# A new opening for a fused attention and expert kernel: other load order, weights cast in two parts, one modulation product moved into block 0

## The chip, the cores and the metric

The kernel runs on one core of one Trainium2 chip. The metric is the time of one execution on the device in microseconds (us), the median of several runs. TensorE is called PE here, VectorE DVE, ScalarE ACT, GpSimd POOL, and SyncE SP. SP only issues DMAs.

## What is computed

```python
mod = (silu(c) @ wmod).reshape(4, 6, 1, -1)          # six modules of 512 columns for each of 4 batches
sa, ca, ga, sb, cb, gb = (mod[:, k] for k in range(6))
h = layernorm(x) * (1 + ca) + sa                     # x: 4 x 2048 x 512
xn = rmsnorm(h) * gamma
q, kv, a = split(xn @ w_qkva.T, 3)                   # 512 columns of each kind
s = scan(sigmoid(a), kv)                             # s[t] = a[t] * s[t-1] + kv[t]
x = x + clip(ga) * (q * s)
h = layernorm(x) * (1 + cb) + sb
x = x + clip(gb) * experts(h)                        # 8 experts, top 2, capacity 320 for each batch
```

## The kernel before

The 8192 tokens are cut into 16 **blocks** of 512 tokens, each of 4 tiles of 128 (TB = 4). The first part of the kernel walks over these blocks. The second part runs the experts, and it isn't touched. Each engine has its own instruction list, written out by hand in `build_program`. Engines wait for one another by counting semaphores, so an instruction that waits holds back all that stands behind it on its engine.

**The opening** comes before block 0. SP loads `wmod` in six modules of 1 MB, the first block of x (1 MB) and the four quarters of the projection weights `wq` (768 KB each). For each module m, `mod_mm(m)` on PE multiplies silu(c) with it (four products, which the profile shows as eight matmuls, since they are fp32), and `mod_copy(m)` on ACT (or one DVE instruction for module 1) takes the row out of PSUM. Modules 1 and 0 are then spread over all partitions by `mod_spread`, and copied from PSUM to `mods`. Module 2 is the gate `ga`, modules 3 and 4 serve the second norm, and module 5 is the gate `gb`, needed by the experts.

ACT's `stats1` computes a block's means (`nm1`) and variances, POOL's `rstd1` takes the inverse root (`rs1`), and DVE's `apply1` makes the normed rows `h1` in two parts: part 0 needs `nm1` and module 1, part 1 needs `rs1` and module 0. ACT's `square` sums the squares of `h1`, POOL's `rnorm1` takes the inverse root, ACT's `hi1` and DVE's `lo1` write the rows as a high and a low fp16 half, and SP's `turn_x` transposes them by DMA (one for each tile) into `xns`.

The weights are cast in the same two halves. DVE's `wq_max` finds the maximum of each quarter; a short exchange over PE (two small products into bank 7) and a chain of small DVE instructions make the scale `gsc`; ACT writes the high halves `wqs[:, 0]`, DVE the low ones.

**A block** on PE is twelve calls of `qkv`, numbered k = 0 to 11: for each quarter c = k // 3 of the 512 columns, the kinds a, kv and q, each of 12 fp16 matmuls of 512 columns. Kind a writes the one bank `bank_a`, and so waits until ACT's `sigmoid` of the quarter before has read it: call k = 6 waits for the second sigmoid. DVE's `mix(c)` is the scan over the block and the product with q; `cga`, the gate, is a factor of that product. For the gate, DVE's `gate(2)` clips module 2, PE's `turn_gate` turns it, and DVE's `gates_done` scales it. The function `step` of each engine gives the order inside a block:

```
ACT, block 0: sigmoid(0), square(block 1), sigmoid(1), hi1(block 1), sigmoid(2), sigmoid(3), stats1(block 2)
DVE, block 0: apply1(block 1, part 0), apply1(block 1, part 1), gates_done, mix(0), lo1(block 1), mix(1), mix(2), mix(3), gate(5)
```

Of the kernel before, what the change touches and what calls it, by code (L numbers as in the profile page):

```python
# [20 lines left out]
P = 128  # L21
# [28 lines left out]
MOD_BANK = {0: 6, 1: 5, 2: 2, 3: 3, 4: 4, 5: 1}  # L50
ROW_DONE = {1: 1, 0: 2, 2: 3, 3: 4, 4: 5, 5: 6}
WQ_LINKS = 12
# [28 lines left out]
def build_program(nc, x, gamma, wq, wr, w1, b1, w2, b2, ct, wmod, out):  # L81
# [4 lines left out]
    with ExitStack() as ctx:  # L86
# [23 lines left out]
        wmod_hi = reg_b[:, :].bitcast(F32)[:, 2 * 2048:].rearrange("p (q n) -> p q n", q=2)  # L110
# [24 lines left out]
        wq_raw = reg_e[:, 2 * TB * D:2 * TB * D + KC * 3 * D].rearrange("p (c e) -> p c e", c=KC)  # L135
        modt = reg_e[:, TB * D:TB * D + 2 * D]
# [388 lines left out]
        def _(sp):  # L525
# [57 lines left out]
            def step(q, j, i):  # L583
                n = 4 * q + j
                if i == 0:
                    for e in range(E // 2):
                        fill(e, 0)
                    turn_x(0, 1)
                    for e in range(E // 2, E):
                        fill(e, 0)  # L590
                if i == 1:
                    sp.wait_ge(s_dch, 14)
                    sp.wait_ge(s_mrow1, 1)
                    sp.dma_start(mod_rows[:, 0:2 * D], modr[0:B, 0:2 * D]).then_inc(s_modw, 16)
# [21 lines left out]
                if i == 0:  # L616
                    for c in range(4):
# [102 lines left out]
            sp.wait_ge(s_modmm, ROW_DONE[5])  # L720
# [14 lines left out]
        def _(pool):  # L735
# [25 lines left out]
            def rnorm1(n):  # L761
                wait_alone(pool, s_sq, TB * n + TB)
                wait_alone(pool, s_xlo, TB * n)
                g.tensor_scalar(rn1[:, :], ss1[:, :], 1e-24 / D / XSCALE ** 2, None, ALU.max).then_inc(s_rna, 1)
                wait(pool, s_rna, n + 1)
                g.tensor_tensor(rn1[:, :], rn1[:, :], half[:, :], ALU.pow).then_inc(s_rn, 1)
# [36 lines left out]
            rnorm1(0)  # L803
# [47 lines left out]
        def _(act):  # L851
# [27 lines left out]
            def square(n):  # L879
                wait(act, s_rn, n)  # L880
# [7 lines left out]
            def hi1(n):  # L888
                wait(act, s_xn, 16 * TB * n)
                wait(act, s_rn, n + 1)  # L890
                for t in range(TB):
                    a.activation(xrow[:, t, 0:D], h1[:, t, :], ACT.Copy, scale=rn1[:, t:t + 1]).then_inc(s_xhi, 1)
# [40 lines left out]
            def mod_copy(m):  # L933
                act.wait_ge(s_modmm, ROW_DONE[m])
                if m == 5:
                    act.wait_ge(s_modc, 1)
# [3 lines left out]
            mod_copy(0)  # L940
            act.wait_ge(s_spread, 2)
            a.activation(mods[:, 0, :], bank[0][:, :], ACT.Copy).then_inc(s_mod0, 1)
            square(0)
            hi1(0)
            act.wait_ge(s_wch0, WQ_LINKS - 4)
            for c in range(KC):
                act.wait_ge(s_wqraw[c], 16)
            for c in range(KC):
                a.activation(wqs[:, 0, c, :], wq_raw[:, c, :], ACT.Copy, scale=gsc[:, c:c + 1]).then_inc(s_wqhi, 1)
            for m in range(2, 6):  # L950
                mod_copy(m)
            stats1(0, 1)
            act.wait_ge(s_wch0, WQ_LINKS)

# [7 lines left out]

            def step(q, j, i):
                n = 4 * q + j
                if has(i, 0):
                    sigmoid(n, 0)
# [15 lines left out]
                if has(i, 0):  # L982
                    sigmoid(n, 2)
                    sigmoid(n, 3)
# [194 lines left out]
        def _(dve):  # L1179
# [27 lines left out]
            def apply1(q, j, part):  # L1207

                n = 4 * q + j
                if part == 0:  # L1210
                    wait(dve, s_nm1, 2 * n + 1)
                    wait(dve, s_xlo, TB * n)
                    if j == 0:
                        wait(dve, s_ma, 16 * q)
                    for t in range(TB):
                        v_.scalar_tensor_tensor(h1[:, t, :], xbuf[:, j, t, :], nm1[:, 0, t:t + 1], mods[:, 1, :],
                                                ALU.add, ALU.mult).then_inc(s_a1, 1)
                else:
                    wait(dve, s_r1, n + 1)
                    if n == 0:  # L1220
                        dve.wait_ge(s_mod0, 1)
                    for t in range(TB):
                        wait(dve, s_a1, TB * n + t + 1)
                        v_.scalar_tensor_tensor(h1[:, t, :], h1[:, t, :], rs1[:, t:t + 1], mods[:, 0, :],
# [64 lines left out]
            dve.wait_ge(s_modmm, ROW_DONE[1])  # L1289
            v_.tensor_scalar(modr[0:B, D:2 * D], bank[MOD_BANK[1]][0:B, :], 1.0, None, ALU.add).then_inc(s_mrow1, 1)  # L1290
            dve.wait_ge(s_spread, 1)
            v_.tensor_copy(mods[:, 1, :], bank[1][:, :]).then_inc(s_modc, 1)
            dve.wait_ge(s_modc, 1)
            apply1(0, 0, 0)

# [5 lines left out]

            wq_max(0)
            apply1(0, 0, 1)
            wq_max(1)
            wq_max(2)
            wq_max(3)
# [7 lines left out]
            lo1(0, 1, 2)  # L1314
# [5 lines left out]
            lo1(0, 2, TB)  # L1320
            for c in range(KC):
                dve.wait_ge(s_wqhi, c + 1)
                v_.scalar_tensor_tensor(wqs[:, 1, c, :], wq_raw[:, c, :], gsc[:, c:c + 1], wqs[:, 0, c, :],
                                        ALU.mult, ALU.subtract).then_inc(s_wqlo, 1)
# [6 lines left out]
            dve.wait_ge(s_modc2, 2)  # L1331
            gate(2)
# [108 lines left out]
            def step(q, j, i):  # L1441
# [21 lines left out]
                if i == 0:  # L1463
                    gates_done()
                if has(i, 0) and j == 0:
                    wait(dve, s_y, KC * n)
                    wait(dve, s_cga, 1 if i == 0 else 0)
                    v_.tensor_copy(cga[:, :], gaS[:, :, q]).then_inc(s_cga, 1)
                    wait(dve, s_cga, 2 * q + 2)
                if has(i, 0):  # L1470
# [500 lines left out]
        def _(pe):  # L1971
            mm, tr = nc.tensor.matmul, nc.tensor.transpose
            pe.sem_inc(s_mm2, 1)
            pe.wait_ge(s_cd, 4 * E + 3)
            pe.wait_ge(s_silc, 1)
# [76 lines left out]
            def qkv(q, j, c, kind):  # L2052
# [12 lines left out]
                if n == 0 and c == 0 and kind == 1:  # L2065
                    pe.wait_ge(s_modc2, 5)
# [39 lines left out]
            pe.wait_ge(s_modc, 1)  # L2106
            attn_steps(step)
# [253 lines left out]
```

## Time and profile before

| | |
|---|---|
| median of 3 runs | 2147.0 us (2145.99 to 2148.63) |
| profiled execution, its time | 2147.44 us |
| its span in the trace | 2145.6 us |
| PE busy | 2113.4 us, 98% |
| DVE busy | 1783.2 us, 83% |
| ACT busy | 1061.7 us, 49% |
| POOL busy | 378.9 us, 18% |

Times in the trace count from the span's start. A row of the timeline gives the start, the duration, the engine, the line of the kernel, the operation, what it writes and reads, and the count of instructions merged into the row; behind it, in brackets, stand the idle time before it and what ended that. A matmul's own duration contains its latency; the pace of a row of many is the row's duration by its count.

### The profile page before, as it was taken

The page shows a single profiled execution, that of the slowest core. Times are in us where ns is not written, and L with a number is a line of the kernel's source. Part 1 is how long each engine was busy: PE and PEld are TensorE (multiplying, and loading weights), DVE is VectorE, ACT ScalarE, POOL GpSimd, SP SyncE. Part 2 cuts the span into 40 slices and gives each one's busy share as a digit, 9 for nine tenths or more (in the row PEclk, how much of TensorE's full clock was granted, in tenths as well). Part 3 has the DMA queues.
Part 4 walks back from the last instruction along what each step waited for, and adds up shares of the span by engine and source line. Part 5 has one row for each costly group of instructions (what it writes and reads, how often), then busy time and mean ns, then how long its engine had stood idle before and what let it go on. Part 6 is the DMA issues. An engine that isn't in the chain of part 4 may idle for free.

```text
span 2145.6 us, 35624 instructions
## 1 busy us (share of the span) xinstructions
PE 2113.4 (98%) x13294; PEld 1257.3 (59%) x13294; DVE 1783.2 (83%) x3029; ACT 1061.7 (49%) x2098; POOL 378.9 (18%) x335
## 2 busy tenths in 40 slices
PE   7999999999999999999999999999999999999998
PEld 2454444445474657656764766576466657656676
DVE  7799989999888887887888779778877987887754
ACT  5465666667372645355253625534461644355150
POOL 1034343433423010100001010101101010100101
PEclk9999999999999999999999999999999999999999
DMA  8899996775675742553274345416434551553202
GB/s 292 246 259 249 243 242 158 177 171 126 160 195 142 207 113 60 145 150 100 33 214 117 81 121 150 124 26 192 105 98 100 171 125 49 168 128 99 40 11 26
DMA packets 353213, 301.05 MB, mean 140 GB/s; under 512 B 242476, under 2 KB 242732, under 8 KB 352529
## 3 DMA queue, kind: packets, MB, share of 16 engines
q1 hardware_dynamic: 331136, 256.63, 43.4%
q0 software_dynamic: 21904, 42.14, 10.3%
q8 instruction: 105, 1.72, 0.3%
q14 instruction: 68, 0.55, 0.1%
HBM read 163.84 MB, written 93.01 MB: 120 GB/s over the span
## 4 chain that ended last, share of the span: by engine, by line
PE 93%; DVE 2%; issue 1%; SPq 0%; DMA 0%; ACT 0%; POOLq 0%; DVEq 0%; ACTq 0%
PE bank L2161 32%; PE bank L2077 20%; PE bank L2231 19%; PE bank L2241 9%; PE bank L2268 5%; PE bank L2259 4%; PE bank L2149 2%; PE bank L2026 1%; DMA reg_e<-reg_e 0%; DVE reg_b L1579 0%; PE bank L2037 0%; PE bank L2039 0%; SPq L581 0%; SPq L573 0%; DVE reg_e L1365 0%
## 5 line engine op out<-in xcount | busy, mean ns | idle before, releaser
L2077 PE MATMUL bank<-reg_c 128*128 128x512 f16 x2296 | 505.2, 379 | 1.0 <-ACT reg_e L961 1.0
L2161 PE MATMUL bank<-reg_e,reg_a 128*128 128x320 f16 x2880 | 447.5, 299 | 0.0
L2231 PE MATMUL bank<-reg_b,reg_c 128*128 128x512 f16 x1920 | 417.3, 379 | 0.9 <-DVE reg_b L1579 0.9
L2077 PEld LDWEIGHTS bank<-reg_c 128*128 128x128 f16 x2296 | 222.3, 98 | 258.3 <-ACT reg_e L961 1.5
L2161 PEld LDWEIGHTS bank<-reg_e,reg_a 128*128 128x128 f16 x2880 | 280.9, 98 | 112.7
L2231 PEld LDWEIGHTS bank<-reg_b,reg_c 128*128 128x128 f16 x1920 | 187.3, 98 | 226.1 <-issue 2.3
L845 POOL DMA_INDIRECT out_dram<-reg_e,midx x79 | 138.8, 1757 | 948.1 <-DVE reg_e L1614 875.2
L2161 PE MATMUL bank<-reg_e,reg_d 128*128 128x320 f16 x1440 | 232.5, 299 | 0.0
L1054 ACT ACTIVATE reg_e<-bank,b1s 128x320 f32<-128x320 f32 x120 | 63.3, 528 | 248.8 <-PE bank L2161 247.9
L2161 PEld LDWEIGHTS bank<-reg_e,reg_d 128*128 128x128 f16 x1440 | 139.7, 98 | 57.6 <-ACT reg_e L1054 4.0
L787 POOL DMA_INDIRECT slot_rows<-reg_e,sli x112 | 129.8, 1159 | 101.1 <-DVE reg_e L1439 60.7
L1649 DVE TENSOR_REDUCE wm<-reg_d 128x1 f32<-128x1024 f32 x112 | 135.6, 1210 | 3.1 <-DMA reg_d<-in_w 3.1
L1704 DVE SCALAR_TENSOR_TENSOR reg_e<-bank,reg_e 128x320 f32<-128x320 f32 x120 | 58.9, 491 | 79.3 <-PE bank L2161 78.3
L1611 DVE SCALAR_TENSOR_TENSOR reg_e<-bank,inv,reg_e 128x512 f32<-128x512 f32 (+1 forms) x81 | 59.9, 740 | 73.7 <-PE bank L2268 41.3
L1124 ACT ACTIVATE reg_e<-reg_e 128x2560 f16<-128x2560 f32 x15 | 35.1, 2337 | 169.1 <-DVE reg_e L1773 169.1
L2161 PE MATMUL bank<-reg_e 128*128 128x320 f16 x720 | 117.4, 299 | 0.0
L2268 PE MATMUL bank<-reg_b,reg_c 128*128 128x512 f16 x512 | 114.4, 379 | 0.0
L1082 ACT ACTIVATE reg_c<-reg_e 128x320 f16<-128x320 f32 x120 | 55.9, 466 | 101.1 <-DVE reg_e L1704 101.1
L961 ACT ACTIVATE reg_e<-bank,iq 128x512 f32<-128x512 f32 x60 | 40.9, 681 | 129.8 <-PE bank L2077 91.5
L2259 PE MATMUL bank<-reg_b,reg_c 128*128 128x512 f16 (+1 forms) x432 | 88.2, 355 | 1.4 <-issue 1.4
L2161 PEld LDWEIGHTS bank<-reg_e 128*128 128x128 f16 x720 | 70.4, 98 | 29.5
L1722 DVE SCALAR_TENSOR_TENSOR reg_a<-reg_d,wsc,reg_a 128x1024 f16<-128x1024 f32 x58 | 71.9, 1279 | 16.8 <-ACT reg_a L1096 16.8
(263 smaller groups left out, 3385.9 us busy)
## 6 DMA issues: line engine op xcount, KB each, us to landing
reg_d<-in_w SPq DMA_DIRECT2D x232, 512.0 KB
slot_rows<-zrow SPq DMA_DIRECT2D x32, 516.0 KB, 4.9
reg_b<-in_x SPq DMA_DIRECT2D x16, 1024.0 KB, 7.4
out_dram<-reg_b SPq DMA_DIRECT2D x16, 1024.0 KB, 7.3
reg_d<-in_w SPq DMA_DIRECT2D x8, 1024.0 KB, 9.6
slot_rows<-zrow SPq DMA_DIRECT2D x32, 129.0 KB, 4.8
reg_d<-in_wmod SPq DMA_DIRECT2D x4, 1024.0 KB, 11.8
reg_e<-mod_rows SPq DMA_DIRECT2D x7, 512.0 KB, 9.5
```

What stands on the lines that cost most here:

```text
L787: g.indirect_dma_start(out=rows, out_offset=bass.IndirectOffsetOnAxis(ap=sli[:, pj % 2, k, t:t + 1], axis=0), in_=rowi[:, pj % 2, t, :], i ...
L845: g.indirect_dma_start(out=out, out_offset=bass.IndirectOffsetOnAxis(ap=midx[:, u, t:t + 1], axis=0), in_=yo[:, n % 4, :], in_offset=None, ...
L1054: a.activation(part_of[:, n % 2, :], u_bank, ACT.Identity, bias=ba[:, p:p + 1], scale=HID_SHIFT).then_inc(s_r0, 1)
L1611: v_.scalar_tensor_tensor(yo[:, n % 4, cols], src, inv2[:, u, kind:kind + 1], b2t[:, cols], ALU.mult, ALU.add).then_inc(s_yd, 1)
L1649: v_.tensor_reduce(wm[:, which, k:k + 1], stage_q[:, q, :, :].rearrange("p c h -> p (c h)"), AX, ALU.max, apply_absolute_value=True).then_ ...
L1722: v_.scalar_tensor_tensor(lo, stage_q[:, q, :, :], wsc[:, 0:1], hi, ALU.mult, ALU.subtract).then_inc(s, 1)
L2077: ins = mm(dst[:, :], wqs[:, ws, kc, e0:e0 + P], xns[:, j % 2, xs, kc, :], start=kc == 0 and xs == 0 and ws == 0, stop=kc == KC - 1 and ws ...
L2161: ins = mm(dst[:, 0:CAP], w[ws][:, c, p * P:(p + 1) * P], xs_of[:, KC * xs + 2 * i + c, j * CAP:(j + 1) * CAP], start=first and c == 0 and ...
L2231: ins = mm(bank_y[i % 2][:, :], hid[:, hs, hc, t * P:(t + 1) * P], w2s[:, ws, hc, :], start=k == 0 and hs == 0 and ws == 0, stop=k == HC - ...
L2241: ins = mm(dst, a_part[:, hs, k, :], b_part[:, ws, k, :], start=first and k == 0 and hs == 1, stop=False, skip_group_check=True)
L2259: ins = mm(dst, hid[:, hs, c, t * P:(t + 1) * P], w2s[:, ws, c, cols], start=j == 0 and hs == 0 and ws == 0, stop=j == HC - 1 and hs == 1, ...
L2268: ins = mm(dst[:, :], hid[:, 0, k, t * P:(t + 1) * P], w2s[:, 0, k, :], start=False, stop=k == HC - 1, skip_group_check=True)
```

## The change

- **Loads.** The first quarter of `wq` goes ahead of x, and the third and fourth each a place forward against the modules. Module 5 is no longer loaded in the opening's batch, but behind `turn_x(0, 0)` and the load of x for block 1, into the place of module 1.
- **Maxima.** DVE takes the first maximum ahead of module 1's row, and the second and third ahead of part 1 of `apply1`.
- **Copies.** For block 0, `apply1` reads the spread modules from PSUM; ACT makes both copies to `mods`, which later blocks of the first batch read.
- **First norm.** `rnorm1` of block 0 is done in two halves, and `lo1` of tiles 1 to 3 stands in one piece ahead of the scale's chain.
- **Weights.** High and low halves are made first for 128 columns of each kind (`wq_hi(0)`, `wq_lo(0)`), then for the other 384 (`wq_hi(1)`, `wq_lo(1)`), which ACT starts behind `mod_copy(4)`. PE waits for these ahead of call k = 3.
- **Order on PE.** 20 matmuls of 128 columns stand ahead of `mod_mm(1)`; the second product of the exchange stands between the halves of `mod_mm(3)`; `mod_mm(5)` moves from the opening to behind call k = 6 of block 0; `turn_gate` moves from behind k = 1 to behind k = 4.
- **Order in block 0.** ACT does sigmoid(0) ahead of `stats1` of block 1 and `mod_copy(5)` between sigmoid(2) and sigmoid(3). DVE does `gates_done`, the copy to `cga` and mix(0) ahead of `apply1` of block 1. Square(block 1) still stands ahead of sigmoid(1) on ACT.

```diff
             load_wmod(1)
+            load_wq(0)
             load_x(0, 0)
             load_wmod(0)
-            load_wq(0)
             load_wq(1)
+            load_wq(2)
             load_wmod(2)
-            load_wq(2)
+            load_wq(3)
             load_wmod(3)
-            load_wq(3)
             load_wmod(4)
-            load_wmod(5)
...
             turn_x(0, 0)
             load_x(0, 1)
+            sp.wait_ge(s_modmm, ROW_DONE[1])
+            load_wmod(5)
...
+            def wq_hi(part):
+
+                for c in range(KC):
+                    a.activation(wq_view(wqs[:, 0, c, :], part), wq_view(wq_raw[:, c, :], part), ACT.Copy,
+                                 scale=gsc[:, c:c + 1]).then_inc(s_wqhi, 1)
...
+            act.wait_ge(s_a1, TB)
+            a.activation(mods[:, 1, :], bank[1][:, :], ACT.Copy).then_inc(s_modc, 1)
+            mod_copy(0)
+            square(0)
+            hi1(0)
+            act.wait_ge(s_h1, TB)
+            a.activation(mods[:, 0, :], bank[0][:, :], ACT.Copy).then_inc(s_mod0, 1)
+            act.wait_ge(s_wch0, GSC_LINKS)
+            for c in range(KC):
+                act.wait_ge(s_wqraw[c], 16)
+            wq_hi(0)
+            for m in range(2, 5):
+                mod_copy(m)
+            wq_hi(1)
+            act.wait_ge(s_wch0, IQ_LINKS)
+            sigmoid(0, 0)
+            stats1(0, 1)
...
             wq_max(0)
+            dve.wait_ge(s_modmm, ROW_DONE[1])
+            v_.tensor_scalar(modr[0:B, D:2 * D], bank[MOD_BANK[1]][0:B, :], 1.0, None, ALU.add).then_inc(s_mrow1, 1)
+            apply1(0, 0, 0)
             wq_max(1)
             wq_max(2)
+            apply1(0, 0, 1)
             wq_max(3)
...
+                if i == 0:
+                    gates_done()
+                    dve.wait_ge(s_cga, 1)
+                    v_.tensor_copy(cga[:, :], gaS[:, :, 0]).then_inc(s_cga, 1)
+                    wait(dve, s_cga, 2)
+                    mix(0, 0, 0)
                 if has(i, 1):
                     apply1(nq, nj, 0)
...
             pe.wait_ge(s_cd, 4 * E + 3)
+            for k in range(20):
+                mm(bank[7][:, 0:P], ones[:, :], ones[:, :], start=True, stop=True)
             pe.wait_ge(s_silc, 1)
...
             mod_mm(2)
-            mod_mm(3)
             pe.wait_ge(s_const, 7)
             pe.wait_ge(s_max0, 3)
             tr(bank[7][0:3, 0:P], mx0[:, 0:3], ident32[:, :]).then_inc(s_maxt, 1)
+            mod_mm(3, 0, 2)
             pe.wait_ge(s_max0, 4)
             mm(bank[7][:, P:P + 3], ones32[0:3, :], maxd[0:3, :], start=True, stop=True).then_inc(s_maxt, 1)
+            mod_mm(3, 2)
             mod_mm(4)
-            pe.wait_ge(s_modc, 1)
-            mod_mm(5)
...
+                if n == 0 and c == 1 and kind == 0:
+                    pe.wait_ge(s_wqhi, 2 * KC)
+                    pe.wait_ge(s_wqlo, 2 * KC)
...
-                    if i == 0 and k == 1:
+                    if i == 0 and k == 4:
                         turn_gate()
+                    if i == 0 and k == 6:
+                        mod_mm(5)
```

## Rows read from the trace of the kernel before

**Rows 1.** The page: busy time, and its 40 slices of 53.6 us.

```profile
PE 2113.4 (98%) x13294; PEld 1257.3 (59%) x13294; DVE 1783.2 (83%) x3029; ACT 1061.7 (49%) x2098; POOL 378.9 (18%) x335
...
PE   7999999999999999999999999999999999999998
```

**Rows 2.** Waits of PE after 38.7 us: total, times, longest.

```profile
PE bank L2077 <- ACT reg_e L961: 1.0, 1, 1.0
PE bank L2026 <- DVE reg_b L1254: 0.8, 1, 0.8
...
PE bank L2026 <- DVE reg_e L1371: 2.1, 1, 2.1
```

**Rows 3.** Timeline of PE, 28 to 75 us.

```profile
28.76 0.27 PE L2000 MATMUL bank<-ident,mx 128*3 128x128 f32 x1 [1.02 <-DVE mx L1308]
...
30.08 8.73 PE L1986 MATMUL bank<-reg_b,silc 128*4 128x512 f32 x16
38.74 1.90 PE L2072 MATMUL bank<-reg_c 128*128 128x512 f16 x8
...
44.02 0.40 PE L2010 MATMUL bank<-ident,reg_a 4*128 4x4 f32 x4
...
48.12 26.07 PE L2077 MATMUL bank<-reg_c 128*128 128x512 f16 x120 [1.00 <-ACT reg_e L961]
```

**Rows 4.** The chain that ended last, merged, from 48 us.

```profile
48.12 23.50 PE bank L2077 x108
```

**Rows 5.** Timeline of DVE and ACT around block 0's first mixes, 46 to 54.5 us.

```profile
49.31 2.74 DVE L1224 SCALAR_TENSOR_TENSOR reg_a<-reg_a,rs,reg_e 128x512 f32<-128x512 f32 x4 [0.24 <-POOL rs L759]
...
51.97 0.23 DVE L1343 TENSOR_SCALAR gaS<-bank,iq 128x16 f32<-128x16 f32 x1
52.08 0.63 ACT L885 ACTIVATE junk<-reg_a 128x512 bf16<-128x512 f32 x1
...
52.71 0.67 ACT L961 ACTIVATE reg_e<-bank,iq 128x512 f32<-128x512 f32 x1
...
53.69 0.75 DVE L1371 SCALAR_TENSOR_TENSOR reg_e<-bank,cga,reg_e 128x512 f32<-128x512 f32 x1
```

**Rows 6.** Timeline: first waits on loads, and block 0's statistics and first norm.

```profile
7.77 5.00 PE L1986 MATMUL bank<-reg_d,silc 128*4 128x512 f32 x8 [7.77 <-DMA reg_d<-in_wmod]
...
10.36 0.63 ACT L865 ACTIVATE reg_a<-reg_b 128x512 bf16<-128x512 f32 x1 [6.39 <-DMA reg_b<-in_x]
...
16.98 1.44 POOL L759 TENSOR_TENSOR rs<-rs,half 128x4 f32<-128x4 f32 x1
18.08 1.75 DVE L1299 TENSOR_REDUCE mxw<-reg_e 128x1 f32<-128x1536 f32 x1
...
20.71 2.74 DVE L1224 SCALAR_TENSOR_TENSOR reg_a<-reg_a,rs,reg_e 128x512 f32<-128x512 f32 x4 [0.88 <-issue]
...
24.14 3.60 PE L1986 MATMUL bank<-reg_d,silc 128*4 128x512 f32 x8 [0.64 <-DMA reg_d<-in_wmod]
```

**Rows 7.** Timeline: the scale's chain, the casts, the transposes, `gate(2)` and what follows it.

```profile
28.46 0.16 DVE L1308 TENSOR_REDUCE mx<-mxw 128x1 f32<-128x4 f32 x1
28.53 0.74 DVE L1230 SCALAR_TENSOR_TENSOR reg_a<-reg_a,rn 128x512 f16<-128x512 f32 x1
...
29.39 5.89 SPq L573 DMA_TRANSPOSE reg_c<-reg_a  x4
...
31.82 5.97 ACT L949 ACTIVATE reg_c<-reg_e,gsc 128x1536 f16<-128x1536 f32 x4 [3.33 <-DVE gsc L1319]
...
40.35 0.15 DVE L1325 SCALAR_TENSOR_TENSOR iq<-is 128x1 f32<-128x1 f32 x1
...
45.56 0.74 DVE L1338 TENSOR_SCALAR reg_a<-reg_a 4x1024 f32<-4x1024 f32 x1
```

**Rows 8.** Windows of PE: busy (instructions), granted clock, DMA share, GB/s.

```profile
28.00:30.00 2.00, 0.50 (x3) 1.00 1.05 387
...
32.00:33.00 1.00, 1.00 (x2) 0.50 1.14 223
```

More of the change, by code:

```diff
@@ L49 @@
 MOD_LINKS = 14
-MOD_BANK = {0: 6, 1: 5, 2: 2, 3: 3, 4: 4, 5: 1}
+MOD_BANK = {0: 6, 1: 5, 2: 2, 3: 3, 4: 4, 5: 5}
 ROW_DONE = {1: 1, 0: 2, 2: 3, 3: 4, 4: 5, 5: 6}
-WQ_LINKS = 12
+WQ_LINKS, GSC_LINKS, IQ_LINKS = 12, 8, 10
 WLINKS = 20
@@ L109, in build_program @@
         xns = reg_c[:, 8 * 3 * D:8 * 3 * D + 16 * BLK].rearrange("p (u s c n) -> p u s c n", u=2, s=2, c=KC)
-        wmod_hi = reg_b[:, :].bitcast(F32)[:, 2 * 2048:].rearrange("p (q n) -> p q n", q=2)
+        wmod_4 = reg_b[:, :].bitcast(F32)[:, 2 * 2048:3 * 2048]
         areg = reg_a[:, :].bitcast(F32)
@@ L133, in build_program @@
         assert at[0] == 15392
-        wq_raw = reg_e[:, 2 * TB * D:2 * TB * D + KC * 3 * D].rearrange("p (c e) -> p c e", c=KC)
-        modt = reg_e[:, TB * D:TB * D + 2 * D]
+        wq_raw = reg_e[:, 0:KC * 3 * D].rearrange("p (c e) -> p c e", c=KC)
+        modt = reg_e[:, 13344:13344 + 2 * D]
         at[0] = 0
@@ L515, in build_program, with wmod_at, rn_at, wq_view @@
         rows16 = rows.bitcast(F16)
+        def wmod_at(m):
+            return (wmod_4 if m == 4 else stage[:, m % 4, :]).rearrange("p (c n) -> p c n", c=KC)
+        def rn_at(n):
+            return n + 2
+        def wq_view(w, part):
+            cols = slice(0, P) if part == 0 else slice(P, D)
+            return w.rearrange("p (k e) -> p k e", k=3)[:, :, cols]
         def slot_cols(v):
@@ L616, in step @@
                 if i == 0:
+                    sp.wait_ge(s_modmm, ROW_DONE[5])
                     for c in range(4):
@@ L759, in rstd1, with rnorm1 @@
                 g.tensor_tensor(rs1[:, :], rs1[:, :], half[:, :], ALU.pow).then_inc(s_r1, 1)
-            def rnorm1(n):
-                wait_alone(pool, s_sq, TB * n + TB)
+            def rnorm1(n, t0=0, t1=TB):
+                wait_alone(pool, s_sq, TB * n + t1)
                 wait_alone(pool, s_xlo, TB * n)
-                g.tensor_scalar(rn1[:, :], ss1[:, :], 1e-24 / D / XSCALE ** 2, None, ALU.max).then_inc(s_rna, 1)
-                wait(pool, s_rna, n + 1)
-                g.tensor_tensor(rn1[:, :], rn1[:, :], half[:, :], ALU.pow).then_inc(s_rn, 1)
+                g.tensor_scalar(rn1[:, t0:t1], ss1[:, t0:t1], 1e-24 / D / XSCALE ** 2, None, ALU.max).then_inc(s_rna, 1)
+                wait(pool, s_rna, rn_at(n) - (t1 < TB))
+                g.tensor_tensor(rn1[:, t0:t1], rn1[:, t0:t1], half[:, t0:t1], ALU.pow).then_inc(s_rn, 1)
             def rstd2(n):
@@ L802, in _ @@
             rstd1(0)
-            rnorm1(0)
+            rnorm1(0, 0, 2)
+            rnorm1(0, 2, TB)
             rstd1(1)
@@ L879, in square @@
             def square(n):
-                wait(act, s_rn, n)
+                wait(act, s_rn, rn_at(n - 1) if n else 0)
                 for t in range(TB):
@@ L889, in hi1 @@
                 wait(act, s_xn, 16 * TB * n)
-                wait(act, s_rn, n + 1)
                 for t in range(TB):
+                    wait(act, s_rn, rn_at(n) - (n == 0 and t < 2))
                     a.activation(xrow[:, t, 0:D], h1[:, t, :], ACT.Copy, scale=rn1[:, t:t + 1]).then_inc(s_xhi, 1)
@@ L934, in mod_copy @@
                 act.wait_ge(s_modmm, ROW_DONE[m])
-                if m == 5:
-                    act.wait_ge(s_modc, 1)
                 a.activation(modr[0:B, m * D:(m + 1) * D], bank[MOD_BANK[m]][0:B, :], ACT.Copy,
                              bias=1.0 if m == 4 else 0.0).then_inc(s_modc2, 1)
[L940 to L953, printed above, removed]
+            def wq_hi(part):
+                for c in range(KC):
+                    a.activation(wq_view(wqs[:, 0, c, :], part), wq_view(wq_raw[:, c, :], part), ACT.Copy,
+                                 scale=gsc[:, c:c + 1]).then_inc(s_wqhi, 1)
             def sigmoid(n, c):
@@ L961, in sigmoid @@
                 a.activation(sig_of(n)[:, c % 2, :], bank_a[:, :], ACT.Sigmoid, scale=iq[:, 0:1]).then_inc(s_sig, 1)
+            act.wait_ge(s_a1, TB)
[15 more added lines that the diff above has]
+            stats1(0, 1)
             def step(q, j, i):
                 n = 4 * q + j
-                if has(i, 0):
+                if has(i, 0) and i > 0:
                     sigmoid(n, 0)
@@ L983, in step @@
                     sigmoid(n, 2)
+                    if i == 0:
+                        mod_copy(5)
                     sigmoid(n, 3)
@@ L1214, in apply1 @@
                         wait(dve, s_ma, 16 * q)
+                    wait(dve, s_spread if n == 0 else s_modc, 1)
                     for t in range(TB):
-                        v_.scalar_tensor_tensor(h1[:, t, :], xbuf[:, j, t, :], nm1[:, 0, t:t + 1], mods[:, 1, :],
+                        v_.scalar_tensor_tensor(h1[:, t, :], xbuf[:, j, t, :], nm1[:, 0, t:t + 1],
+                                                bank[1][:, :] if n == 0 else mods[:, 1, :],
                                                 ALU.add, ALU.mult).then_inc(s_a1, 1)
@@ L1220, in apply1 @@
                     if n == 0:
-                        dve.wait_ge(s_mod0, 1)
+                        dve.wait_ge(s_spread, 2)
+                    else:
+                        wait(dve, s_mod0, 1)
                     for t in range(TB):
                         wait(dve, s_a1, TB * n + t + 1)
-                        v_.scalar_tensor_tensor(h1[:, t, :], h1[:, t, :], rs1[:, t:t + 1], mods[:, 0, :],
+                        v_.scalar_tensor_tensor(h1[:, t, :], h1[:, t, :], rs1[:, t:t + 1],
+                                                bank[0][:, :] if n == 0 else mods[:, 0, :],
                                                 ALU.mult, ALU.add).then_inc(s_h1, 1)
@@ L1287, in wlink @@
                 dve.wait_ge(s_wch0, wlinks[0])
[L1289 to L1294, printed above, removed]
             def wq_max(c):
@@ L1300, in wq_max, with wq_lo @@
                                  apply_absolute_value=True).then_inc(s_wmax, 1)
+            def wq_lo(part):
+                for c in range(KC):
+                    dve.wait_ge(s_wqhi, KC * part + c + 1)
+                    v_.scalar_tensor_tensor(wq_view(wqs[:, 1, c, :], part), wq_view(wq_raw[:, c, :], part), gsc[:, c:c + 1],
+                                            wq_view(wqs[:, 0, c, :], part), ALU.mult, ALU.subtract).then_inc(s_wqlo, 1)
             wq_max(0)
-            apply1(0, 0, 1)
+            dve.wait_ge(s_modmm, ROW_DONE[1])
+            v_.tensor_scalar(modr[0:B, D:2 * D], bank[MOD_BANK[1]][0:B, :], 1.0, None, ALU.add).then_inc(s_mrow1, 1)
+            apply1(0, 0, 0)
             wq_max(1)
             wq_max(2)
+            apply1(0, 0, 1)
             wq_max(3)
@@ L1313, in _ @@
             v_.tensor_scalar(maxd[0:3, :], ident32[0:3, 0:3], mxr[0:3, 0:1], None, ALU.mult).then_inc(s_max0, 1)
-            lo1(0, 1, 2)
+            lo1(0, 1, TB)
             dve.wait_ge(s_maxt, 2)
@@ L1319, in _ @@
             wlink(v_.tensor_scalar(gsc[:, :], gams[:, :], sc0[:, 0:1], None, ALU.mult))
[L1320 to L1324, printed above, removed]
+            assert wlinks[0] == GSC_LINKS
             wlink(v_.scalar_tensor_tensor(iq[:, 0:1], is0[:, 0:1], 1.0 / XSCALE, is0[:, 2:3], ALU.mult, ALU.mult))
             wlink(v_.tensor_tensor(iq[:, 1:2], iq[:, 0:1], iq[:, 0:1], ALU.mult))
+            assert wlinks[0] == IQ_LINKS
+            wq_lo(0)
+            wq_lo(1)
+            dve.wait_ge(s_modc2, 2)
+            gate(2)
             wlink(v_.tensor_scalar(wrs[:, 0, :, :], wrr[:, :, :], sc0[:, 1:2], None, ALU.mult))
@@ L1330, in _ @@
             assert wlinks[0] == WQ_LINKS
-            dve.wait_ge(s_modc2, 2)
-            gate(2)
             scb = modr[0:B, 3 * D:5 * D]
@@ L1449, in step @@
                     wait(dve, s_cga, 2 * q + 3)
+                if i == 0:
+                    gates_done()
[3 more added lines that the diff above has]
+                    mix(0, 0, 0)
                 if has(i, 1):
@@ L1462, in step @@
                     add_y(n - 1, pj, 3)
-                if i == 0:
-                    gates_done()
-                if has(i, 0) and j == 0:
+                if has(i, 0) and j == 0 and i > 0:
                     wait(dve, s_y, KC * n)
-                    wait(dve, s_cga, 1 if i == 0 else 0)
                     v_.tensor_copy(cga[:, :], gaS[:, :, q]).then_inc(s_cga, 1)
                     wait(dve, s_cga, 2 * q + 2)
-                if has(i, 0):
+                if has(i, 0) and i > 0:
                     mix(q, j, 0)
@@ L1982, in mod_mm @@
             def mod_mm(m, c0=0, c1=KC):
-                wm = (stage[:, m, :] if m < 4 else wmod_hi[:, m - 4, :]).rearrange("p (c n) -> p c n", c=KC)
-                pe.wait_ge(s_wmod[m], 16)
+                wm = wmod_at(m)
+                if c0 == 0:
+                    pe.wait_ge(s_wmod[m], 16)
+                if m == 5:
+                    pe.wait_ge(s_mrow1, 1)
                 for c in range(c0, c1):
@@ L2087, in step @@
                         qkv(q, j, k // 3, k % 3)
+                    if i == 1 and k == 0:
+                        pe.wait_ge(s_modc2, 5)
                     if k < 2 and has(i, -1):
@@ L2106, in _ @@
             pe.wait_ge(s_modc, 1)
+            pe.wait_ge(s_a1, TB)
+            pe.wait_ge(s_h1, TB)
             attn_steps(step)
```

7 lines of the change are left out of this document (3 added, 4 removed).

## The prediction

> **What bounds the kernel now.** The page comes first. PE is busy for 98% of the span, and of its 40 slices only the first and the last stand below 9 [rows 1]. So a time is won or lost where PE idles, or where PE gets other work to do. The change touches the first 75 us, inside the first two slices. The list of waits gives what PE loses behind its first projection matmul: 1.0 us on the first sigmoid and 0.8 us on the first sum of block 1; of the later waits the longest is 2.1 us [rows 2]. PE's timeline then gives the two marks that I measure from: call k = 0 starts at 38.74, right at the end of modules 4 and 5 (30.08 + 8.73 = 38.81) [rows 3], and call 11 ends at 48.12 + 23.50 = 71.62 [rows 4]. The 23.50 us hold nine calls, so a call takes 2.61 us. From the first call to the end of the last it is 71.62 - 38.74 = 32.9 us. I call the start of call 0 S. The question is what S becomes, and what stands between S and the end of call 11.
>
> **When the projection starts (S).** Loads first. From 7.77 (module 1 in) to 24.14 (module 3 in, PE waiting for it) seven loads land, four of 1 MB and three of 768 KB, so 16.4 us for 6.25 MB, or 2.6 us for 1 MB and 2.0 us for a quarter of wq [rows 6]. In the new order x stands behind one quarter: its first ACT row moves from 10.36 to 12.3, and `rs1`, which ended at 16.98 + 1.44 = 18.4, to 20.4. Module 3 lands at 7.8 + 4 x 2.6 + 4 x 2.0 = 26.2.
>
> DVE: the means come some 2.8 us behind x, at 15.2. Part 0 (2.74) then ends at 17.9, two maxima of 1.75 at 21.4, part 1 at 24.1, the last maximum at 25.9, and the small reduction over the four at 26.1. Before, that ended at 28.46 + 0.16 = 28.6 [rows 6, 7]. So 2.5 us are won here, because a maximum and a copy have left the path. From there to the scale it was 31.82 - 28.6 = 3.2 us. Now `lo1` of all four tiles (0.74 each) stands in it, two more than before, as does half of module 3 on PE. I get the scale at 31, and at 32.5 if PE is at the low clock.
>
> PE: the small transpose at 26.4 to 26.6, half of module 3 (half of 3.60), the second small product (0.4), the other half, and module 4 (3.60). That ends at 34.2. Before, the same pattern, small products between idle stretches, was followed by two modules in 8.73 instead of 2 x 3.60 = 7.20, so 1.5 us are lost [rows 3, 6]; the window view shows PE busy for 0.50 of 2 us from 28 to 30, and the clock granted at 0.50, the lower of its two levels, 1.2 instead of 2.4 GHz, from 32 to 33 [rows 8]. With that again, PE is free at 35.7. The operand: `lo1` of tile 0 ends at 26.8, and the four transposes took SP 5.89, so the last is issued by 32.8. The trace has no landing time for them. They were in at 38.74 at the latest, 3.5 us behind the end of the last issue at 35.28 [rows 3, 7]; so the bounds are 32.8 and 36.3. The cast of the first 128 columns of each kind is a quarter of the elements, so 1.5 of the 5.97 us, and some 2.1 us with the fixed time of four instructions (an estimate); it ends at 33 to 35: covered. S is between 34.2 and 36.3. I take 35.0, between PE without and with the low clock. **Won: 38.7 - 35.0 = 3.7 us.** The split first norm, the 20 matmuls ahead of module 1 (PE idles there until 7.77 anyway) and the second copy on ACT lie behind loads or DVE and cost nothing; without that cover the copy would be 0.6 us of ACT.
>
> **Call 6 waits for a chain that now begins later.** This is the step that decides. Call 6 needs `bank_a`, so sigmoid(1). On ACT, sigmoid(1) stands behind square(block 1), and so behind the whole `apply1` of block 1 on DVE. Before, that was the first thing in DVE's block 0: part 1 ended at 49.31 + 2.74 = 52.05, sigmoid(1) at 52.71 + 0.67 = 53.38 [rows 5], and call 6 wanted it at 48.12 + 3 x 2.61 = 55.9. It had 2.5 us to spare. Now DVE does `gates_done` and mix(0) first, and `gates_done` waits for `turn_gate`, which PE does only behind call 4. The chain, from S:
> - five calls 13.05, and four small transposes 0.40 [rows 3, 4]: 13.45
> - `gates_done`, the copy, scan and product: 51.97 to 53.69 + 0.75, so 2.47 [rows 5]: 15.9
> - `apply1` of block 1, two parts of 2.74: 21.4
> - last row of `h1` to the end of sigmoid(1), 52.05 to 53.38, so 1.33: 22.75.
>
> PE is ready for call 6 at 13.45 + 2.61 = 16.05. It idles for 6.7 us, where it stood before 1.0 us for the whole block. Nothing in this chain depends on how early S is: each link is a wait on the link before it. Whether DVE itself is ready for `gates_done`: the high halves of the other 384 columns start behind module 4's copy, S + 0.6, and are three quarters of 5.97 plus overheads, 4.7; the last low half follows 1.4 later; then come `gate(2)` and the rest, 46.30 - 40.35 = 5.95 [rows 7]. That is S + 12.7, just under the 13.45. Statistics of block 1 on ACT start at S + 6 and end at S + 12, well before part 1. The new wait ahead of call 3 (S + 7.8) is for the low halves, at S + 6.7: covered with 1.1 to spare.
>
> **Module 5 inside block 0.** It was 3.6 us ahead of S, and is 3.6 us behind call 6. It is PE work on the path in both places: what S won is in part this. Its load (issued behind the transposes, SP being free at about 33, 7 us) is in at 41, long before.
>
> **The clock over the wait.** After 6.7 idle us I expect the low clock at call 6, and take the loss of the one stretch that the trace has, 1.5 us; the bounds are 0 and, for a stretch twice as long, 3.0. The trace shows one wait of 1.0 us in the middle of calls, and the calls after it ran at full pace [rows 2, 4]. The Trainium skill's TensorE: Matmul & The Clock Gate, Part 1, says that the throttled half rate is the default and that activity releases it, and that idleness brings it back; by that rule the loss comes, and the forecast's change is +7.0, where without it it would be +5.5. The fall that the window view shows agrees with it.
>
> **The sum.** From S to the end of call 11: 22.75 + six calls 15.7 + module 5 3.6 + clock 1.5 = 43.55, against 32.9 before: +10.7. Less the 3.7 won at S: **+7.0 us**. Behind call 11 nothing differs: mix(3), `gate(5)`, `apply1` of block 2 and the first sum follow in the same order, so the 0.8 us wait stays. The profiled execution took 2147.44, 0.4 over the median of the runs, its span 2145.6; on the median 2147.0 the forecast is 2154.0.
>
> **Rivals.**
> 1. *The low clock costs nothing* at the wait (and S is 34.2, also without it): +9.2 - 4.5 = +4.7, so 2151.7. For it: the drop depends on the moment at which PE idles. Against it: 6.7 us is far more idleness than stood before the fall in rows 8.
> 2. *Later waits absorb a part.* DVE and SP get ahead while PE stands; PE's waits behind block 1, the 2.1 us one first, could shrink by some 2 us: +5.0, so 2152.0. Against it: those waits are for DVE's work on PE's own latest output, and they move with PE.
> 3. *The wait doesn't come*, which ends on the other side: sigmoid(1) is there at S + 16.05. Then it is -3.7 at S, -1.0 for the old sigmoid wait, +3.6 for module 5: -1.1, so 2145.9, no measurable change. This decides if the chain's 22.75 is really under 16.1, that is if mix(0) and `apply1` don't stand ahead of square and sigmoid(1). The order in the code speaks against it. To be faster by over 0.2% (4.3 us, about what a measurement of this kernel can tell from no change) S would have to be below 32 as well.
> 4. *S is late*: transposes land at the late bound, 36.3, or the low halves hold call 3 by 1 us: +8.3 to +9, so 2155.8.
>
> **Numbers.** The forecast 0.5, rival 1 0.15, rival 2 0.1, rival 3 0.08, rival 4 0.17. The range reaches from rival 1 with some absorption, +3, to rival 4: 2150.0 to 2156.5. Faster 0.03, the same 0.13 (rival 3 and the low tails of 1 and 2), slower 0.84.
>
> **What would show it.** Right: call 0 near 35; one PE wait of 6 to 7 us, 16 us behind it, ended by ACT's sigmoid; DVE's scan ahead of block 1's `apply1`; a granted clock of 0.50 behind that wait; eight fp32 matmuls behind the next call; the end of call 11 near 78.6. Wrong: call 6 starting without a wait, S under 33 or over 37, or marks of later blocks that are less far behind than call 11.

## The result, and the profile after

The changed kernel takes 2156.0 us (median of 6 runs, 2153.3 to 2158.1), the kernel before 2148.3 in the same comparison: ratio 1.0035, 95% interval 1.0026 to 1.0045. That is 7.6 us slower; the forecast was +7.0 and 2154.0, in a range of 2150.0 to 2156.5. The profiled execution was the slowest of the six, 2158.14 us, its span 2156.4.

PE's timeline of the changed kernel, from the last product of the opening to the first transposes of block 1, answers to [rows 3]:

```profile
30.46 3.60 PE L2025 MATMUL bank<-reg_b,silc 128*4 128x512 f32 x8
33.99 1.90 PE L2113 MATMUL bank<-reg_c 128*128 128x512 f16 x8
35.73 11.39 PE L2118 MATMUL bank<-reg_c 128*128 128x512 f16 x52
47.05 0.41 PE L2048 MATMUL bank<-ident,reg_a 4*128 4x4 f32 x4
47.39 2.76 PE L2118 MATMUL bank<-reg_c 128*128 128x512 f16 x12
56.73 5.08 PE L2118 MATMUL bank<-reg_c 128*128 128x512 f16 x12 [6.58 <-ACT reg_e L965]
61.74 3.60 PE L2025 MATMUL bank<-reg_d,silc 128*4 128x512 f32 x8
65.27 15.71 PE L2118 MATMUL bank<-reg_c 128*128 128x512 f16 x72
80.82 1.04 PE L2064 MATMUL bank<-ident,reg_e 128*128 128x128 f32 x8
...
85.26 1.24 PE L2064 MATMUL bank<-ident,reg_e 128*128 128x128 f32 x8 [0.81 <-DVE reg_b L1283]
```

Call 0 starts at 33.99 instead of 38.74. Call 6, at 56.73, has waited 6.58 us, and then takes 5.0 us instead of 2.6. Module 5 (61.74) follows, then five calls of block 0 and one of block 1 in the row of 72. The chain that ended last gives the end of the five (start, duration, what):

```profile
65.33 13.07 PE bank L2118 x60
```

So call 11 ends at 78.4 instead of 71.62 [rows 4], 6.8 us later. The wait of 0.81 in block 1 is the same as before [rows 2].

What holds call 6 stands in the timeline of DVE and ACT, against [rows 5]:

```profile
47.56 0.23 DVE L1374 TENSOR_SCALAR gaS<-bank,iq 128x16 f32<-128x16 f32 x1 [0.81 <-PE bank L2048]
47.84 0.17 DVE L1484 COPY cga<-gaS 128x4 f32<-128x4 f32 x1
48.04 1.22 DVE L1396 TENSOR_TENSOR_SCAN reg_e<-reg_e,bank 128x512 f32<-128x512 f32 x1
...
49.30 0.75 DVE L1402 SCALAR_TENSOR_TENSOR reg_e<-bank,cga,reg_e 128x512 f32<-128x512 f32 x1
...
49.96 2.73 DVE L1241 SCALAR_TENSOR_TENSOR reg_a<-reg_b,nm,reg_e 128x512 f32<-128x512 f32 x4
...
52.61 2.73 DVE L1252 SCALAR_TENSOR_TENSOR reg_a<-reg_a,rs,reg_e 128x512 f32<-128x512 f32 x4
53.44 0.63 ACT L900 ACTIVATE reg_a<-reg_a 128x512 bf16<-128x512 f32 x1 [7.86 <-issue]
...
56.01 0.67 ACT L965 ACTIVATE reg_e<-bank,iq 128x512 f32<-128x512 f32 x1
```

ACT stands idle for 7.86 us at the first square (from 45.6 to 53.4), with sigmoid(1) behind it, whose input had been in PSUM since call 3, which ended at about 44.4. The windows of PE (busy, instructions, granted clock, DMA share, GB/s) show what the wait does to the clock:

```profile
52.00:54.00 2.00, 0.00 (x0) 1.00 0.32 72
54.00:56.00 2.00, 0.00 (x0) 0.66 1.05 404
56.00:58.00 2.00, 1.27 (x4) 0.50 1.06 384
58.00:60.00 2.00, 2.00 (x6) 0.50 1.08 359
60.00:62.00 2.00, 2.00 (x6) 0.64 1.05 254
62.00:64.00 2.00, 2.00 (x6) 1.00 0.99 192
```

PE has done nothing since 50.1. The clock still reads 1.00 up to 54, falls to the lower level, 1.2 GHz, between 54 and 56, and is back near 61.

The two profiled executions differ by more than 6.8 us at the end, 10.8 in span. Between 80 and 660 us one window of 10 us differs in its clock: 320 to 330 reads 0.83 here, and all of them read 1.00 before. The transposes in it begin 7.6 us late (323.86 against 316.26), those of the next block 9.25 (359.35 against 350.10). They stand behind a wait of 2 us, and take 1.62 us instead of 1.09:

```profile
323.86 1.62 PE L2064 MATMUL bank<-ident,reg_e 128*128 128x128 f32 x8 [1.93 <-DVE reg_e L1402]
```

The kernel before has the wait as well, 2.13 us, without the fall of the clock. Other executions show it with and without the fall too: in b2 below the transposes take 1.64 us behind 2.06 us of waiting, in a1 1.09 us behind 2.07. So the fall at this place isn't the change's. This is why I compare medians and, inside the traces, the first 80 us.

### The profile page after: what moved, and what is told of

It reads as the page before. It is cut to its first block, busy times and chain, and to the rows that moved or that the text cites. A ratio compares the mean times of both kernels' runs of the same rounds, so it can differ in the third digit from the quotient of the medians.

```text
span 2156.4 us, 35686 instructions
## 1 busy us (share of the span) xinstructions
PE 2120.2 (98%) x13314; PEld 1259.8 (58%) x13314; DVE 1782.9 (83%) x3032; ACT 1062.7 (49%) x2103; POOL 377.0 (17%) x337
## 4 chain that ended last, share of the span: by engine, by line
PE 89%; DVE 4%; issue 2%; DMA 2%; SPq 1%; POOL 1%; ACT 0%; POOLq 0%; DVEq 0%; another core or an unknown queue 0%
PE bank L2208 31%; PE bank L2118 20%; PE bank L2278 17%; PE bank L2288 9%; PE bank L2315 5%; PE bank L2306 4%; PE bank L2064 1%; DMA reg_d<-in_w 1%; DMA reg_d<-in_wmod 1%; POOL slot_rows L828 1%; PE bank L2196 1%; DVE wmx L1557 1%; PE bank L2025 0%; DMA reg_e<-reg_e 0%; DVE reg_e L1277 0%
```

## The experiments

Each kernel was timed in five rounds against the kernel before. The before of its own group stands beside each time; the groups had 2147.3, 2147.8 and 2148.5.

**a1: `apply1` of block 1 first again.** On DVE, in the changed kernel:

```diff
-                if i == 0:
-                    gates_done()
-                    dve.wait_ge(s_cga, 1)
-                    v_.tensor_copy(cga[:, :], gaS[:, :, 0]).then_inc(s_cga, 1)
-                    wait(dve, s_cga, 2)
-                    mix(0, 0, 0)
                 if has(i, 1):
                     apply1(nq, nj, 0)
...
+                if i == 0:
+                    gates_done()
...
+                    mix(0, 0, 0)
```

> The changed kernel with one thing undone: in block 0, gates_done, the copy to cga and mix(0) stand behind both parts of apply1 of block 1 on DVE, as before. Theory (the wait of call 6 is the chain gate, mix(0), apply1, square, sigmoid(1)): apply1 runs from 46.8 to 52.0, sigmoid(1) ends at 53.4 instead of 56.7, PE waits 3.2 us instead of 6.6, call 11 ends 3.3 to 5.8 us earlier (the latter if the low clock is gone too): 2150.2 to 2152.7 against 2156.0 for the changed kernel. Rival (module 5 in block 0 and the later blocks cost the time, the order doesn't): the wait only moves to mix(0), and the time stays at 2156.

Measured: 2151.3 against 2147.3, ratio 1.0013 (1.0003 to 1.0023), so +4.0 by the medians (+2.8 by the ratio) where the changed kernel had +7.6. PE's timeline:

```profile
53.67 4.13 PE L2118 MATMUL bank<-reg_c 128*128 128x512 f16 x12 [2.72 <-ACT reg_e L965]
```

The wait is 2.72 us instead of 6.58, and even this short one costs 1.4 us more in the call behind it. So as long as sigmoid(1) stands behind the square, DVE's order makes 3.9 of the 6.6 us. The other 2.7 come with the earlier call 0 (34.82 here against 38.74): DVE gets to `apply1` no sooner than in the kernel before (46.90 against 46.34).

**a2: sigmoid(1) ahead of the square.** On ACT, in the changed kernel:

```diff
+                if i == 0:
+                    sigmoid(n, 1)
                 if has(i, 1):
                     square(n + 1)
...
-                if i == 0:
-                    sigmoid(n, 1)
```

> The changed kernel with one ACT instruction moved: sigmoid(1) of block 0 ahead of square of block 1. Theory: the wait of call 6 goes (call 6 at about 50.1 us), so does the low clock, call 11 ends at 69.3 instead of 78.4, 2.3 us earlier than in the kernel before: about 2147, the kernel before at 2148.3. Rival 1 (another wait takes its place, such as the transposes of block 1 or the second scan, which still stand behind apply1 and hi1): part of the 9 us stays, 2148 to 2152. Rival 2 (the order costs nothing): 2156.

Measured: 2145.8 against 2147.3, ratio 0.9995 (0.9986 to 1.0004). Moving this one call ahead takes away what the change cost. PE's timeline has no wait there:

```profile
48.03 0.41 PE L2048 MATMUL bank<-ident,reg_a 4*128 4x4 f32 x4
48.37 5.35 PE L2118 MATMUL bank<-reg_c 128*128 128x512 f16 x24
53.66 3.60 PE L2025 MATMUL bank<-reg_d,silc 128*4 128x512 f32 x8
57.19 15.71 PE L2118 MATMUL bank<-reg_c 128*128 128x512 f16 x72
```

Calls 5 and 6 run in one piece. Call 11 ends at 57.19 + 13.07 = 70.3, 1.4 us ahead of the kernel before, 8.1 ahead of the changed one. No other wait takes the place. Call 0 began at 34.99 in this execution, 1.0 later than in the changed kernel; c3 comes back to that.

**a3: the wait filled.** Ahead of call 6 of block 0, in the changed kernel:

```diff
+                    if i == 0 and k == 6:
+                        for _ in range(110):
+                            mm(bank[6][:, 0:P], ones[:, :], ones[:, :], start=True, stop=True)
```

> The changed kernel with 110 matmuls of 128 columns on a constant, into an unused bank, put into the wait ahead of call 6 of block 0 (6.1 us at full pace in a wait of 6.6). The wait stays. Theory (the idle time brings the low clock, which costs 2.4 us in call 6, 5.1 instead of 2.6): call 6 takes 2.6, call 11 ends 2.4 us earlier, 2153.5 against 2156.0. Rival (the clock is not set by the idle time): call 6 stays at 5.1, and the time at 2156.

Measured: 2152.0 against 2147.3, ratio 1.0021 (1.0012 to 1.0030), +4.7 instead of +7.6.

```profile
50.30 6.30 PE L2129 MATMUL bank<-ones 128*128 128x128 f16 x110
57.03 2.76 PE L2118 MATMUL bank<-reg_c 128*128 128x512 f16 x12 [0.43 <-ACT reg_e L965]
```

Call 6 starts as late as before, but takes 2.7 us. The granted clock reads 1.00 from 50 to 66. From its start to module 5 it is 59.73 - 57.03 = 2.7 us, against 61.74 - 56.73 = 5.0. So the low clock was a cost of the idle time, 2.3 us, and useless work in the wait saves it. The medians moved by 2.9.

**b1: the order alone, in the kernel before.** `gates_done`, the copy and mix(0) ahead of `apply1` on DVE, as in the change, and on PE:

```diff
-                    if i == 0 and k == 1:
+                    if i == 0 and k == 4:
                         turn_gate()
```

> The kernel before with the order alone changed: gates_done, the copy to cga and mix(0) ahead of apply1 of block 1 on DVE, turn_gate behind call 4. Module 5, the loads, maxima and casts stay as before. Theory: call 0 stays at 38.7, sigmoid(1) ends near 63, PE waits 6.7 us at call 6, and call 6 costs 2.4 more at the low clock: call 11 ends near 81, +9.5 us, 2157.8 against 2148.3. Rival (the cost came with module 5 and the other parts): 2148 to 2149.

Measured: 2156.4 against 2147.3, ratio 1.0039 (1.0025 to 1.0053), +9.1. PE's timeline:

```profile
38.11 1.89 PE L2075 MATMUL bank<-reg_c 128*128 128x512 f16 x8 [0.28 <-DMA reg_c<-reg_a]
...
65.49 20.71 PE L2080 MATMUL bank<-reg_c 128*128 128x512 f16 x84 [6.58 <-ACT reg_e L961]
```

The wait is 6.58 us, to the digit what it is in the changed kernel, though call 0 starts 4 us later and neither module 5 nor the casts moved. The seven calls behind it take 20.7 us instead of 18.3, the low clock again. In this execution two more things came: the wait for sigmoid(0) ahead of call 3 was 2.07 us and not 1.0, and calls 3 and 4 behind it took 7.0 us instead of 5.2. Call 11 so ends at 83.6, not at the 81 that I had worked out; the median is less far off than that. The order alone makes a loss as large as the whole change's: +9.1 and +7.6, with intervals that overlap. That the rest of the change won a part back isn't shown by this pair; a2, c3 and d2 bear on it.

**c1: module 5 into the wait.** In the changed kernel:

```diff
-                    if i == 0 and k == 6:
+                    if i == 0 and k == 5:
                         mod_mm(5)
```

> The changed kernel with module 5's product ahead of call 6 of block 0 instead of behind it, so inside the wait of 6.6 us. Theory (the wait is set by ACT and DVE, and module 5 is plain PE work behind it): call 6 still starts near 57, its wait shrinks to 3.0 us, call 7 follows at once, and 3.5 us go, with up to 2.4 more from the clock: 2150.1 to 2152.5, the changed kernel at 2156.0. Rival (module 5 behind call 6 is hidden by other engines anyway): no change, 2156.

Measured: 2150.4 against 2147.8, ratio 1.0008 (0.9999 to 1.0018), +2.5.

```profile
50.92 3.60 PE L2025 MATMUL bank<-reg_d,silc 128*4 128x512 f32 x8
57.57 21.20 PE L2118 MATMUL bank<-reg_c 128*128 128x512 f16 x84 [3.05 <-ACT reg_e L965]
```

Call 6 starts no earlier against call 0 (57.57 - 34.85 = 22.7), but module 5 no longer follows it. The 3.6 us were on the path. The clock falls in the 3.05 us as well: seven calls in 21.2 instead of 18.3. So against call 0 the end of call 11 comes 3.1 us earlier than in the changed kernel; the medians moved by 5.1 (7.6 to 2.5), and what the other 2 us are, the trace of the first 80 us doesn't show.

**c3: no matmuls ahead of module 1.** a2's kernel without the 20 matmuls:

```diff
-            for k in range(20):
-                mm(bank[7][:, 0:P], ones[:, :], ones[:, :], start=True, stop=True)
```

> The kernel with sigmoid(1) first, without the 20 matmuls ahead of module 1. Theory (they run while PE waits for its first load, and module 1's row isn't what part 0 of apply1 waits for): call 0 within 0.3 us of the same place, 2145.8. Rival (they raise the clock for module 1): call 0 is 1 us or more later, 2147.

Measured: 2144.1 against 2147.8, ratio 0.9987 (0.9978 to 0.9997). Call 0 starts at 34.27. Module 1's product, of c3 first and then of a2 and of the changed kernel, from their timelines:

```profile
7.49 5.87 PE L2023 MATMUL bank<-reg_d,silc 128*4 128x512 f32 x8 [7.49 <-DMA reg_d<-in_wmod]
```

```profile
7.49 6.42 PE L2025 MATMUL bank<-reg_d,silc 128*4 128x512 f32 x8 [0.78 <-DMA reg_d<-in_wmod]
```

```profile
7.60 4.89 PE L2025 MATMUL bank<-reg_d,silc 128*4 128x512 f32 x8 [0.84 <-DMA reg_d<-in_wmod]
```

With the 20 matmuls it took from 4.2 to 6.4 us in seven traces, without them 5.0 to 6.1 in five, and 3.6 is full pace. The two sets overlap, and no trace shows what the same execution would have taken without them. The times show no gain either: the intervals of a2 and c3 overlap, and so do those of d1 and d2 below. Where it took 6.42 (a2), part 0 of `apply1` waited for it and started at 15.91, not 14.92, and call 0 came 1.0 us later. So module 1 is on the path when it is slow, which I had ruled out, but the matmuls are no sure cure.

Module 1 isn't all of it. In a1 and c1 it took only 4.2 and 4.3 us, and call 0 still came at 34.82 and 34.85. There module 0's product was the slow one, 5.29 us at a granted clock that fell to 0.50 between 16 and 18, and part 1 of `apply1` began 1.0 us late, at 21.8, right behind the spread of module 0 (20.61 + 1.12 in a1).

**c4: x first.** a2's kernel with the load of x ahead of the first quarter of `wq`, as before:

```diff
-            load_wq(0)
             load_x(0, 0)
+            load_wq(0)
```

> The kernel with sigmoid(1) first, and x again ahead of the first quarter of wq. Theory (DVE's row of maxima, module 1's row and apply1 is the path, not x): x is there 2 us earlier, but DVE's first maximum, ahead of module 1's row, waits 2 us longer, part 0 of apply1 starts 0.7 later, call 0 0.7 later: 2146.5. Rival (x is the path): call 0 is up to 2 us earlier, 2144.

Measured: 2148.0 against 2147.8, ratio 1.0003 (0.9995 to 1.0012). The interval overlaps a2's. Call 0 starts at 35.52, later than in every other run of the new opening (33.99 to 34.99), though module 1 took only 4.69 us here. Two things add up in this execution. The timeline shows x in 2 us earlier, and DVE waiting for the quarter, with module 1's row behind it:

```profile
10.00 0.63 ACT L880 ACTIVATE reg_a<-reg_b 128x512 bf16<-128x512 f32 x1 [6.12 <-DMA reg_b<-in_x]
...
11.90 1.75 DVE L1321 TENSOR_REDUCE mxw<-reg_e 128x1 f32<-128x1536 f32 x1 [2.61 <-DMA reg_e<-in_wq]
...
13.57 0.67 DVE L1333 TENSOR_SCALAR reg_a<-bank 4x512 f32<-4x512 f32 x1
...
15.35 5.29 PE L2025 MATMUL bank<-reg_d,silc 128*4 128x512 f32 x8
...
22.53 2.72 DVE L1252 SCALAR_TENSOR_TENSOR reg_a<-reg_a,rs,bank 128x512 f32<-128x512 f32 x4 [0.96 <-issue]
```

Beside that, module 0's product took 5.29 us, as in a1 and c1, and part 1 of `apply1` stood 0.96 us until its spread was done (21.32 + 1.12). Against those two the order of the loads leaves 0.7 us of call 0 (35.52 against 34.82 and 34.85), which is what was expected of it.

**d1: gate(5) into an idle place.** a2's kernel, with mix(3) moved behind gate(5) and the two instructions that follow it in DVE's `step`:

```diff
-                if has(i, 0):
-                    mix(q, j, 3)
                 if i == 0:
                     dve.wait_ge(s_modc2, 5)
...
                     dve.wait_ge(s_cd, 4 * E + 7)
+                if has(i, 0):
+                    mix(q, j, 3)
```

> The kernel with sigmoid(1) first, and DVE's gate(5) with the two instructions behind it ahead of mix(3) of block 0 instead of behind it. DVE is idle there for 4.4 us, and 2.6 us leave the path from mix(3) over apply1 of block 2 to the first sum of block 1. Theory: PE's wait of 0.8 us in block 1 goes, with the 0.2 us between the next transposes: 2144.8 against 2145.8, and against 2147.3 for the kernel before. Rival (the wait has another reason): it stays, 2145.8.

Measured: 2144.1 against 2147.8, ratio 0.9982 (0.9972 to 0.9991). The transposes of block 1 follow without a wait:

```profile
33.99 1.89 PE L2113 MATMUL bank<-reg_c 128*128 128x512 f16 x8
...
72.60 2.75 PE L2118 MATMUL bank<-reg_c 128*128 128x512 f16 x12
75.19 1.04 PE L2064 MATMUL bank<-ident,reg_e 128*128 128x128 f32 x8
```

They begin 2.59 us behind call 1 of block 1 instead of 3.57: 1.0 us won in the trace. This kernel beats the kernel before, by 3.7 us, and so the changed one too. Its interval overlaps a2's, so the times don't show what the move alone is worth.

**b2: the same in the kernel before**, and **d2: d1 without the 20 matmuls**.

> The kernel before with gate(5) and the two instructions behind it ahead of mix(3) of block 0, and nothing else. Theory: PE's wait of 0.8 us in block 1 goes, and 1.0 us in all: 2146.8, where d1 stood at 2144.1; the rest of d1's gain is the new opening's. Rival (d1's gain came from this move alone): 2144.

> The d1 kernel without the 20 matmuls ahead of module 1. Theory: they are worth nothing, call 0 at 34.0 to 35.0 like in all runs of the new opening, 2144 to 2145. Rival (they help when the clock comes up in time for module 1): 2145 or more, and call 0 at 34.5 or later.

Measured: b2 2147.8 against 2148.5, ratio 0.9999 (0.9990 to 1.0008). The wait of 0.8 us is gone from its trace, but 1 us is too little to tell in the times. d2 2144.2 against 2148.5, ratio 0.9979 (0.9970 to 0.9988), the same as d1. b2 and d2 differ by the whole change less the 20 matmuls, with sigmoid(1) first, and their intervals don't meet. So the new opening does win, once call 6 doesn't wait: 3.6 us between these two medians.

## Why the prediction was right

**The start of the projection.** Forecast 35.0, with 34.2 as the early bound; measured 33.99, just outside. I had taken half of the loss to a low clock behind the small products, which didn't come here: the windows from 24 to 36 us read 1.00. That half of module 3 between the small products kept it away isn't shown. b1 and b2 have the old opening, and the two modules behind the small products took 7.03 us there and not 8.73. This is b1:

```profile
30.48 0.38 PE L2005 MATMUL bank<-maxd,ones 3*128 3x3 f32 x2 [0.74 <-DVE maxd L1313]
30.79 7.03 PE L1989 MATMUL bank<-reg_b,silc 128*4 128x512 f32 x16
```

In the changed kernel the low clock came at another place, in module 2's product, which took 4.88 us; the windows from 20 to 24 read 0.62 and 0.52. It cost call 0 nothing, since module 3's load was waited for behind it (0.27 us at 26.63).

```profile
21.28 4.88 PE L2025 MATMUL bank<-reg_d,silc 128*4 128x512 f32 x8 [1.08 <-DMA reg_d<-in_wmod]
```

So S moves from run to run, in both openings: 37.69 to 38.74 in three traces of the old one, 33.99 to 34.99 in eight of the new one (c4 left out). The mean of the eight is 34.5, half way between the forecast and 33.99; the profiled execution of the changed kernel has the earliest of them, with d1. An early S didn't help the old kernel: in b2 call 0 began at 37.69, but call 3 waited for sigmoid(0), and call 11 ended at 48.18 + 23.50 = 71.7, where it ends in the kernel before.

The transposes came early too: in a2 PE waited 0.78 us for them, and they landed at 34.99, 2.3 us behind SP's last issue. In the changed kernel PE and the transposes come out together.

**The chain to call 6.** Forecast 22.75 us from call 0 to call 6, measured 56.73 - 33.99 = 22.74; the wait 6.7, measured 6.58. The runs that kept both orders repeat it: 22.71 in a3, 22.72 in c1, and the same wait of 6.58 in b1, behind calls with waits of their own. DVE was ready at 46.76, S + 12.8, and waited 0.81 us for `turn_gate`, as worked out. Rival 3, no wait, is what a2 built: 2145.8 there, 2145.9 forecast for it.

**The low clock** is the term that was sized too small: 1.5 us forecast, 2.4 measured in call 6 (5.0 against 2.6), 2.3 against a3. I had taken the loss of an fp32 stretch behind two short idle times; here twelve fp16 matmuls ran at half pace nearly throughout. Rival 1, no loss, falls with it. The Trainium skill's TensorE: Matmul & The Clock Gate, Part 1, has the rule (throttled by default, released by activity, back after idleness), and the windows and a3 agree with it. From call 0 to the end of call 11 it took 44.4 us where 43.55 were forecast, and call 0 came 1.0 us earlier than forecast. These two errors cancel, and that is luck: 10.7 - 3.7 = 7.0 forecast, 44.4 - 32.9 - 4.75 = 6.8 measured, at the end of call 11. The mechanism is as forecast.

**Module 5** cost 3.53 us behind call 6 as forecast; c1 shows it on the path.

**Later waits** absorbed nothing (rival 2): the marks of block 2 stand 6.8 us behind (114.82 against 108.03), those of later blocks 7 to 10. The marks of blocks 4 to 7 stand 7.5 behind (183.23 against 175.69 in block 4). Why the medians differ by 7.6 and not 6.8 stays open; the interval, 1.0026 to 1.0045 or 5.6 to 9.7 us, holds both. A part of it may be that the profiled execution of the changed kernel had an early S: with the mean of 34.5 call 11 would end at 34.5 + 44.4 = 78.9, 7.3 behind (an estimate).

**What I had wrong** without harm: that the clock of module 1 can't matter. A slow product of module 1 (a2) or of module 0 (a1, c1) each moved call 0 by up to 1 us.

## What to carry to other kernels

An engine's instruction list is a chain too: when work is moved ahead on one engine, list what stands behind it on that engine, and what stands behind *that* on the next. Here mix(0) was brought ahead on DVE and pushed back another block's norm. A sigmoid that needed neither stood behind that norm on ACT; it had always stood there, and it had 2.5 us to spare. Moving it ahead was worth 8.1 us in the trace, more than the 4.75 by which call 0 had become earlier. Whether mix(0) ahead of the norm is worth anything once the sigmoid is out of the way, no run shows: all kernels with sigmoid(1) first keep it there. An idle stretch of PE can cost more than its length: behind the wait of 6.58 us the calls lost another 2.4 to the low clock. So ready work belongs into the wait, not behind it, which was worth 3.1 us in c1's trace and 5.1 by the medians.

## What was not expected of the hardware

- Waits of 2.7 and 3.05 us already brought the low clock for the work behind them (a1, c1: 1.4 and 2.9 us lost). The shorter wait of 3.05 us cost more than the one of 6.58 (2.4 lost); why, no run shows.
- Waits of about 2 us went either way. Behind 1.93 us (changed kernel, 1.65 us lost), 2.06 (b2) and 2.07 (b1, calls 3 and 4 in 7.0 us instead of 5.2) the clock fell; behind 1.85 (d2), 2.07 (a1) and 2.13 (kernel before) it did not.
- 20 matmuls in 2.3 us, ending 0.5 to 0.9 us ahead of the first product, did not reliably raise its pace: 4.2 to 6.4 us for eight that take 3.6 at full pace.
